# Two of four block transposes moved behind the next row maximum, with four smaller moves, in a fused cross attention and mixture-of-experts kernel

## The reference, cut to what matters

```python
# 16 batches of 128 tokens, width 256; 16 heads of 64; keys are 128 context rows and 128 latent rows
x = x + xcond(ctx_1024, _layernorm(x), cond, cond, ...)
#   x, lat = layer_norm(ctx) * w + b, (layer_norm(latents) * w + b) * (1 + scale) + shift
#   q = lat @ Wq.T;  k, v = split(concat(x, lat) @ Wkv.T)          per head
#   w = softmax(q @ k.T / sqrt(64));  out = (w @ v) @ Wo.T
x = x + ffn(_layernorm(x), router, w1, w3, w2, ws1, ws3, ws2)
#   shared expert for every token, plus one of 8 routed experts (top 1) for each token
```

## Time and profile before

| | us |
|---|---|
| median of 3 runs | 697.55 (696.97 to 699.01) |
| the profiled execution, device time | 700.39 |
| its span, first to last instruction | 698.6 |
| PE busy | 670.5 (96% of the span) |
| DVE busy | 490.7 (70%) |
| ACT busy | 427.7 (61%) |
| POOL busy | 329.2 (47%) |

### The profile page before, as it was taken

How to read it: one execution, slowest core, us unless ns; L and a number is a source line. 1 busy time by engine, 2 the same in 40 slices (tenths; PEclk the granted TensorE clock), 3 DMA queues, 4 the chain that set the end, 5 groups by cost and what they waited for, 6 DMA issues and landing times. The chain is left out here.

```text
span 698.6 us, 17836 instructions
## 1 busy us (share of the span) xinstructions
PE 670.5 (96%) x5705; PEld 611.1 (87%) x5706; DVE 490.7 (70%) x1062; ACT 427.7 (61%) x1166; POOL 329.2 (47%) x528
## 2 busy tenths in 40 slices
PE   8799999999999999999997999999999999999997
PEld 8779888888888897888886998898899999999997
DVE  7688778888898888888875876447536676535353
ACT  4888777878878878788776894333325454222222
POOL 2745645645546465454557562019430345333333
PEclk9899999999999999999999999999999999999999
DMA  7644555765756665565554541300758999888870
GB/s 276 181 115 128 164 152 152 196 178 159 201 163 177 181 180 164 182 185 171 166 156 139 146 115 49 117 1 18 198 171 275 291 342 313 259 260 266 253 243 8
DMA packets 84192, 123.82 MB, mean 177 GB/s; under 512 B 30572, under 2 KB 47598, under 8 KB 83888
## 3 DMA queue, kind: packets, MB, share of 16 engines
q1 hardware_dynamic: 69328, 98.76, 46.3%
q0 software_dynamic: 11808, 24.42, 12.2%
q10 hardware_dynamic: 3008, 0.03, 0.3%
HBM read 69.77 MB, written 22.70 MB: 132 GB/s over the span
## 5 line engine op out<-in xcount | busy, mean ns | idle before, releaser
L1165 PE MATMUL PS<-BIG 128*128 128x256 f32 (+1 forms) x1302 | 233.4, 333 | 18.1 <-DVE BIG L935 11.6
L1165 PEld LDWEIGHTS PS<-BIG 128*128 128x128 f32 x1302 | 188.5, 191 | 48.7 <-DVE BIG L935 17.1
L741 ACT ACTIVATE PR<-PS,NMX 128x256 f32<-128x256 f32 x256 | 120.9, 497 | 67.3 <-DVE NMX L948 67.2
L2251 PE MATMUL PS<-XST,W 128*128 128x128 f32 x1012 | 116.7, 275 | 0.0
L2251 PEld LDWEIGHTS PS<-XST,W 128*128 128x128 f32 x1012 | 115.0, 192 | 0.1
L750 ACT ACTIVATE PR<-PR,RINV 128x256 f32<-128x256 f32 x256 | 111.6, 531 | 0.3 <-DVE RINV L955 0.3
L960 DVE STREAM_TRANSPOSE PR<-PR 128x512 f32<-128x512 f32 x124 | 80.9, 686 | 4.5 <-ACT PR L750 3.2
L948 DVE TENSOR_REDUCE NMX<-PS 128x4 f32<-128x1024 f32 x64 | 74.5, 1197 | 0.0
L535 POOL DMA_DIRECT2D PT<-PR x128 | 64.3, 508 | 15.1 <-issue 8.4
L1746 POOL DMA_INDIRECT out_x<-YS,WHO x23 | 31.2, 1356 | 84.3 <-DVE YS L2113 74.7
L544 POOL DMA_DIRECT2D QF<-queries x92 | 50.9, 558 | 32.2 <-DMA queries<-QT 32.1
(11 more groups left out here) (193 smaller groups left out, 1131.2 us busy)
## 6 DMA issues: line engine op xcount, KB each, us to landing
PT<-PR SPq DMA_DIRECT2D x368, 64.0 KB, 2.6
W<-in_w SPq DMA_DIRECT2D x29, 640.0 KB, 4.5
W<-in_w SPq DMA_DIRECT2D x21, 768.0 KB
PT<-PR POOLq DMA_DIRECT2D x128, 64.0 KB, 2.5
queries<-QT SPq DMA_DIRECT2D x23, 256.0 KB, 2.2
QF<-queries POOLq DMA_DIRECT2D x92, 64.0 KB, 2.5
turned<-CXN SPq DMA_DIRECT2D x15, 256.0 KB, 2.9
INT<-turned POOLq DMA_DIRECT2D x56, 64.0 KB, 2.7
```

The source lines that it names most:

```text
L741: last = act.activation(probs, logits, ACT.Exp, bias=NMX[:, g, own, p % 2:p % 2 + 1], accum_out=SUM[:, p, own:own + 1])
L1165: last = pe.matmul(dst, stat(s, k), mov(m, k), start=n == 0, stop=n == len(todo) - 1)
L2251: last = pe.matmul(h[:, P * c:P * (c + 1)], lhs13(W13[par], k, c), XST[par][:, :, k, :], start=k == 0, stop=k == KD - 1)
```

## The change

Five moves, none of which adds or removes an instruction that computes:

1. DVE: in the steady batches the last two `transpose_blocks` of a half no longer stand at its end but in the next half, between `row_max(h, 0)` and `row_max(h, 1)`.
2. ACT and DVE, second half: `k_hi(h+1, 0, 0)` stands ahead of `o_hi(h-2)`, and `k_lo(h+1, 0, 0)` ahead of `o_lo(h-2, 1)` and `expert_input`.
3. PE, first half: `output_projection(b-2)` stands ahead of `q_turned(h+2)`.
4. POOL, batches 13 and 14: all pieces of the weight split stand behind `keep_probs` and `load_inputs`.
5. POOL, batch 15: the first four pieces stand ahead of `rstd`.

```diff
@@ POOL, batch
                 keep_probs(b - 1, 1)
                 if norm:
                     norms(b + 2)
+                early_parts = HP if between and not following else 0
+                for j in range(early_parts):
+                    between(j)
                 rstd(3, 1, v_mv3, p_ve3, p_rs3, b - 1)
                 if ahead:
                     load_queries(2 * b + 2, 0)
-                early_parts = HP if between else 0
-                for j in range(early_parts):
-                    between(j)
                 keep_probs(b, 0)
@@ ACT, half_1
                 exps(h, b, 1, 1, final)
+                if not final:
+                    k_hi(h + 1, 0, 0)
                 if not first:
                     o_hi(h - 2, b - 1, 1)
-                if not final:
-                    k_hi(h + 1, 0, 0)
@@ DVE, half_0
                 row_max(h, 0)
+                if not first and not second and not switch:
+                    for p in (2, 3):
+                        transpose_blocks(h - 1, 1, p)
...
-                for p in (1, 2, 3):
+                for p in (1, 2, 3) if first or second or last else (1,):
                     transpose_blocks(h, 0, p)
@@ DVE, half_1
-                for g in range(2):
-                    row_max(h, g)
+                row_max(h, 0)
+                if not first and not second and not final:
+                    for p in (2, 3):
+                        transpose_blocks(h - 1, 0, p)
+                row_max(h, 1)
                 if not first:
                     o_lo(h - 3, 0)
...
+                if not final:
+                    k_lo(h + 1, 0, 0)
                 if not first:
                     o_lo(h - 2, 1)
                 if not first and not second:
                     expert_input(b - 2)
-                if not final:
-                    k_lo(h + 1, 0, 0)
...
-                if not final:
+                if first or second:
                     for p in (2, 3):
                         transpose_blocks(h, 1, p)
@@ PE, half_0
+                if not first and not second:
+                    output_projection(b - 2)
                 if ahead:
                     q_turned(h + 2, b + 1, 0, 1 - par)
-                if not first and not second:
-                    output_projection(b - 2)
```

More of the change, by code:

```diff
@@ L1017, in last_pt, with half_0 @@
                 last.then_inc(v_pt, 1)
-            def half_0(b, par, first=False, second=False, switch=False, norm=True, turned=False, ahead=False):
+            def half_0(b, par, first=False, second=False, switch=False, norm=True, turned=False, ahead=False, last=False):
                 h = 2 * b
@@ L1061, in half_1 @@
                     expert_input(b - 2)
-                if not final:
-                    k_lo(h + 1, 0, 0)
-                else:
+                if final:
                     last_values(0)
@@ L1096, in batch @@
             def batch(b, par, first=False, second=False, switch=False, last=False, norm=True, turned=False, ahead=False):
-                half_0(b, par, first, second, switch, norm, turned, ahead)
+                half_0(b, par, first, second, switch, norm, turned, ahead, last)
                 half_1(b, par, first, second, switch, last, norm, ahead)
```

## The result

| | before | after |
|---|---|---|
| median, us | 697.68 (11 runs) | 701.94 (11 runs, 699.33 to 704.27) |
| ratio, 95% interval | | 1.0065 (1.0049 to 1.008) |
| the profiled execution, device time | 700.39 | 702.17 |
| its span | 698.6 | 700.4 |
| `modulate` of batch 3, 12, 13 starts at | 116.54, 343.65, 373.51 | 115.25, 346.88, 372.72 |

The change costs 4.3 us (3.4 to 5.6 by the interval). One of the 11 executions before took 1326.86 us and is left out of the ratio; the other ten took 696.95 to 700.12 us. The two profiled executions differ by 1.8 us only: before's lay 2.7 us above its median, after's 0.2. Part of the rest is seen in a run further down: before's profiled execution was already late at `modulate` of batch 2 (88.81, against 86.89 in the kernel with parts 4 and 5 alone, whose order is the same up to there).

A forecast was written before the change was run, and what follows sets the result against it. PE was the fullest engine, but a loop through SP and POOL, nearly as long, was to become the bound. Loop 5.4, batch 13 -2.8, `logits(29)` +1.3 and clock +1.4 gave +5.3 us: 702.8 us, range 696.5 to 705.5.

The forecast's parts named there:

- The loop through SP and POOL: Round trip from `modulate` through SP and POOL back to `modulate`: grows from 24.89 to 26.05 us, period up 0.82 us.
- The landing: Stretch from SP's store of queries to POOL's loads: stays at 3.93 us per batch.
- rival B: Half of the 1.16 us shift is swallowed, as by an earlier landing: 697.0 us, chance 0.20.
- Rival C: All of the shift is swallowed, loop stays at 24.89 us: 691.3 us, the most possible gain; chance 0.12.
- PE's own work: PE in the attention loop: would need 24.45 us per batch once its 0.78 us of waits go.
- The rule of the Trainium skill: Queries' store: 2.0 us plus bytes over 436 GB/s, 2.6 us; would make the changed loop 24.7 us.
- The start: Batches 2 and 3: `modulate` of batch 3 could start at 114.6, not 116.54, 1.9 us ahead.
- Batch 13: Interval from batch 12 to 13: 27.1 us instead of 29.86, giving back 2.8 us; `modulate` 2.6 us late.
- The delay of `logits(29)`: Behind batch 13's `modulate`: 12.5 us instead of 11.2, as POOL's loads queue behind the split; 1.3 us more.
- The clock: Batch 14: PE idles 3.7 us before `logits(29)`, then slow matmuls cost 1.4 us, bounds 0 to 2.8.
- Parts 2 and 3: Attention loop: PE's two waits of 0.78 us per batch go, but cost and gain are nothing, as the loop ends later.
- The sum: Whole kernel: 5.4 - 2.8 + 1.3 + 1.4 = +5.3 us, put on the median of 697.55: 702.8 us.

The follow-up runs named there:

- the first experiment: The changed kernel with the last two transposes of a second half back at that half's end: 689.08 us, ratio 0.9879 to the kernel before.
- the third experiment: The changed kernel with SP's two clearing zero stores of a batch issued behind the store of the queries: 687.20 us, ratio 0.9842 to the kernel before.
- the kernel that joined the split with both gains: The changed kernel with second-half transposes back, clearing stores late, and three weight-split pieces moved to batch 14 ahead of `keep_probs(27)`: 693.16 us, ratio 0.9937.
- both gains: The changed kernel with the second half's transposes back at its end and SP's clearing stores late: 686.37 us, ratio 0.9849 to the kernel before.
- the last kernel of that section: The changed kernel with second-half transposes back, clearing stores late, and three weight-split pieces in batch 14 behind `keep_probs(27)`: 687.91 us, ratio 0.9867.
- the three-piece split: The changed kernel with three of the six weight-split pieces moved to batch 14, behind `load_queries(29, 1)` and ahead of `keep_probs(27)`: 702.97 us, ratio 1.0081.
- a third clear: The changed kernel with one more 128.5 KB zero store per batch behind SP's two clearing stores: 711.64 us, ratio 1.019 to the kernel before.

## Why the prediction was right, and where it was off

**The loop through SP and POOL** was the right mechanism, and the step "SP can't start `move_probs` before" the right link: 4.13 us forecast, 4.13 measured. Shortening the way through SP in two different places gave 13 and 15 us back, lengthening it cost 10, and part 1 alone brings the whole loss. The waits that show it were shorter than forecast: DVE's for INT 1.2 us a time where I had 1.4, and PE's for `q_lo` 1.2 where I had 1.6.

**The landing** was the mis-sized term: 3.93 us taken, 3.45 measured, 0.48 us too much in each of nine intervals. That looks like rival B, the landing swallowing part of the shift, but the runs speak against it for all but 0.1 us. Averages of the nine intervals, one execution each:

| kernel | block behind `modulate` | landing | period |
|---|---|---|---|
| before | 2.97 | 3.93 | 25.23 |
| parts 4 and 5 alone (same order in the loop) | 2.96 | 3.54 | 25.16 |
| parts 2 and 3 alone | 2.96 | 3.53 | 25.29 |
| part 1 alone | 4.13 | 3.46 | 25.61 |
| parts 1 to 3 | 4.13 | 3.34 | 25.61 |
| the whole change | 4.13 | 3.45 | 25.74 |

Without the shift the landing is 3.5 us in two kernels, with it 3.3 to 3.5; 3.93 was high in that one execution, at an unchanged order. So the loop before had 0.7 us of room in those two executions and not 0.34, the shift of 1.16 us overran it by 0.5, and the period grew by 0.4 to 0.5 where I had 0.82. (The 2.65 us for INT should have read 2.72, which makes the room in before's own execution 0.28.) Rival C's bound, that "the loop before the change has room for 0.34 us per batch only", goes with it: with the block at 2.98 us, the first experiment ran at 24.28.

**PE's own work** was taken as 24.45 us per batch. In the kernels that hardly wait it is busy for 23.9 us, so the first and the third experiment could fall below the period of 24.5 us that I had as the least. Why it is busy for 24.2 to 24.6 us in the slower kernels is not shown.

The rule of the Trainium skill ("DMA: Bandwidth & Descriptors", "Anatomy of one DMA — SWDGE (gpsimd) path") gives 2.6 us for these 256 KB, an estimate from that page. It is stated for DMAs that GpSimd issues, while SP issues this one, and the prediction set it against a stretch that holds 0.70 us more than the landing. With the clears out of the way the store itself landed in 2.01 to 2.05 us in all nine intervals, 0.6 us below the rule. Behind two zero stores it took 0.7 us more on average (2.75), behind three 1.2 us more (3.19).

**The start** was wrong: "the loop starts 1.9 us ahead". Batch 3's `modulate` at 116.54 was late in that one execution. Without part 1 it came at 113.82 and 114.06, in the three kernels of the table with part 1 at 114.41 to 115.44. The term was a loss of about 1 us, not a gain of 1.9.

**Batch 13** took 25.84 us, not 27.1. The slow stretch of SP in the kernel before (10.27 us) was an event of that execution; it was 9.44 here. `modulate` of batch 13 thus came 0.8 us early and not 2.6 late.

**The delay of `logits(29)`** was right: 12.22 us behind `modulate` (12.5 predicted, 11.2 before). **The clock** too: 1.6 us (1.4). The idle times ahead of it were 1.16 and 2.54 us, where I had 3.7 in one piece.

**Parts 2 and 3.** That they "gain nothing, as the loop ends later" came true, but the reason was incomplete. I counted two loops, PE's and SP's. Alone, parts 2 and 3 gain nothing either (ratio 1.0009), as DVE and ACT hold a third of 25.2 us. Part 1 takes 1.2 us out of that loop per pair and puts 1.16 us into SP's with the second pair. That is why half of part 1 is worth 8.6 us together with the other parts (1.5 to 1.7 of them from POOL's split, if it is worth there what it is elsewhere), and the whole of it costs 4.3.

**The sum.** The parts, each against the kernel before timed beside it, roughly add up:

| kernel | median, us | ratio to before |
|---|---|---|
| part 1 alone | 703.80 | 1.0107 |
| parts 2 and 3 alone | 698.24 | 1.0009 |
| parts 4 and 5 alone | 695.37 | 0.998 |
| parts 1, 2 and 3 | 703.61 | 1.009 |
| all | 701.94 | 1.0065 |

1.07 + 0.09 - 0.20 = 0.96%, against 0.65% (0.49 to 0.80) for all; each part's interval is 0.12 to 0.19 wide to either side. Parts 2 and 3 don't worsen part 1.

That 702.8 came so close to 701.94 was partly luck. Between the two profiled executions the forecast was 5.3 us and the measured difference 1.8: the start came 0.6 us later than forecast, the nine intervals took 2.8 us less, batch 13 took 1.2 less, the delay of `logits(29)` 0.3 less, the slow clock 0.2 more. The medians are 4.3 us apart only since before's execution lay 2.7 us above its own. Against more usual executions of the kernel before, the landing made the loop 3 to 4 us too dear and the start was 3 us too cheap, and both errors came from taking one execution as the ground. What delays single executions in this way stays open.

## What to carry to other kernels

Look for every closed loop that comes back to the same instruction one batch later, also through queues and half-idle engines, and write down its length; a move is worth what it takes out of the longest one, less what it puts into the next. Idle time of the fullest engine is no stake until the loop behind it is known: here the moves aimed at PE's 0.78 us per batch alone gained nothing, and two transposes behind one row maximum were worth 1.0.

An in-order list of DMA issues is an engine with a length of its own. Stores that nobody waits for belong behind the one that closes a loop. When such a list or POOL's is touched, price each instruction queued behind the moved one, not only the one for whose sake it was moved.

## What the runs showed of the hardware

- A store's landing depends on what its queue has ahead of it. From issue to landing the 256 KB of queries took 2.01 to 2.05 us without the two zero stores directly ahead (nine intervals), 2.5 to 3.2 on average with two, 3.19 with three. At two zero stores it differed by 0.7 us between executions of kernels with the same order on SP (3.22 before, 2.48 in the first experiment); why is not settled.
- POOL's loads started 0.70 us behind the landing that they waited for, in all nine intervals before and after.
- Two idle times of PE shortly after one another didn't always bring the clock down. It fell behind 1.16 and 2.54 us in the changed kernel (0.62 and 0.53 granted), and behind only 0.35 and 1.74 us in the kernel that joined the split with both gains (0.74, then 0.50). It stayed at 1.00 behind 0.33 and 2.63 us in the last kernel of that section, and behind 1.14, 2.10 and 2.02 us in the three-piece split:

```profile
384.00:386.00 2.00, 1.69 (x26) 1.56 (x28) 1.86 (x7) 2.00 (x6) 1.40 (x3) 1.00 0.66 164
388.00:390.00 2.00, 0.08 (x2) 0.11 (x4) 1.95 (x3) 0.06 (x1) 0.55 (x1) 1.00 0.66 137
390.00:392.00 2.00, 2.00 (x33) 1.83 (x34) 0.53 (x1) 2.00 (x8) 1.92 (x6) 1.00 0.94 294
```

  A term for the clock is thus a chance as much as a cost: 0 in two of these four kernels, 1.6 us in the changed one, 2.4 us over the 64 products in the one that joined the split with both gains.
- The kernels held by the loop through DMAs scattered more: 699.3 to 704.3 us after (11 runs) and 708.1 to 713.5 with a third clear (6), against 685.3 to 687.4 with both gains (4) and 687.5 to 688.2 with the split behind `keep_probs` as well (4). The runs are few.
